# Graph layers on one core: ScalarE's share of the tile loads, and a fourth slot for them

## The reference

```python
# layer 0
u = par_u[0] * par_u[1] * (diag_u[:, None] * ego_u @ W_u) + ego_u   # nodes 0..2047
i = par_i[0] * par_i[1] * (diag_i[:, None] * ego_i @ W_i) + ego_i   # the other 3072
e = jnp.concatenate([u, i], axis=0)
h = adj @ (adj.T @ e)
out = (h - mu) * jax.lax.rsqrt(var + LN_EPS) * ln_gamma + ln_beta + res
x = _layernorm(x + out)
# layer 1 (K = 4)
Tx_prev1 = L_scaled @ x                 # L_scaled is adj
out = Tx_prev2 @ weight[0] + Tx_prev1 @ weight[1]
for k in range(2, K):
    Tx_curr = 2.0 * (L_scaled @ Tx_prev1) - Tx_prev2
    out = out + Tx_curr @ weight[k]
x = _layernorm(x + out + bias)
```

## Time and profile before

| | |
|---|---|
| median of 3 runs | 1394.04 us (1385.07 to 1394.7) |
| profiled execution | 1395.09 us, span 1393.3 us |
| TensorE busy | 1201.9 us (86%) |
| VectorE busy | 883.3 us (63%) |
| ScalarE busy | 181.7 us (13%) |
| moved by DMA | 371.78 MB, mean 267 GB/s |
| mean granted TensorE clock | 0.949 of full speed |

### The profile page before, as it was taken

One profiled execution on the slowest core, in us unless ns is written; L12 is line 12 of the kernel. 1 busy time (PEld: TensorE's weight loads), 2 busy tenths in 40 slices (PEclk: granted clock), 3 DMA queues, 4 the chain that ended last, 5 costly groups with the idle time before them and its releaser, 6 DMA issues.

```text
span 1393.3 us, 14444 instructions
## 1 busy us (share of the span) xinstructions
PE 1201.9 (86%) x5324; PEld 514.1 (37%) x5324; DVE 883.3 (63%) x940; ACT 181.7 (13%) x353; POOL 62.5 (4%) x98
## 2 busy tenths in 40 slices
PE   5789989979989889787497899999999999678785
PEld 4344444434444344333132333334434444122221
DVE  2467655765767667566366677666556666677783
ACT  1112212212212122130001001000010000010111
POOL 0820000000000000000000000000000000011111
PEclk9899999989999999998789999999999999989898
DMA  8999999999999999869799999999999999999992
GB/s 246 248 253 275 254 281 256 273 258 278 238 280 248 281 248 267 178 122 180 148 232 268 291 332 319 299 308 298 261 251 330 317 333 310 337 311 324 322 340 76
DMA packets 414968, 371.78 MB, mean 267 GB/s; under 512 B 12892, under 2 KB 413572, under 8 KB 414932
## 3 DMA queue, kind: packets, MB, share of 16 engines
q1 hardware_dynamic: 301332, 258.33, 70.7%
q10 hardware_dynamic: 110880, 110.11, 28.9%
q0 software_dynamic: 2720, 2.86, 1.0%
HBM read 369.94 MB, written 1.31 MB: 266 GB/s over the span
## 4 chain that ended last, share of the span: by engine, by line
PE 35%; SPq 34%; DMA 15%; DVE 9%; issue 4%; ACT 1%; ACTq 1%; POOL 0%; DVEq 0%
PE bank L1024 24%; SPq L312 21%; SPq L323 12%; DMA raw<-in_adj 8%; DMA shared<-in_adj 6%; DVE turned L452 5%; PE bank L1075 2%; PE bank L1037 2%; PE bank L1053 1%; DVE shared L452 1%; PE bank L884 1%; PE bank L1180 1%; PE bank L1087 1%; DVE stats L414 1%; ACTq L265 1%
## 5 line engine op out<-in xcount | busy, mean ns | idle before, releaser
L1024 PE MATMUL bank<-turned,terms 128*128 128x512 f32 x680 | 316.9, 619 | 44.6 <-DVE turned L452 44.0
L452 DVE STREAM_TRANSPOSE turned<-raw 128x2048 f32<-128x2048 f32 x93 | 213.2, 2301 | 130.0 <-DMA raw<-in_adj 76.4
L884 PE MATMUL bank<-shared 128*64 128x256 f32 x1600 | 224.3, 404 | 48.0 <-DMA shared<-in_adj 47.7
L472 DVE STREAM_TRANSPOSE shared<-shared 32x512 f32<-32x512 f32 x320 | 224.9, 703 | 25.0 <-ACT t_cols L692 20.6
L1024 PEld LDWEIGHTS bank<-turned,terms 128*128 128x128 f32 x680 | 131.5, 198 | 221.0 <-issue 189.5
L460 DVE STREAM_TRANSPOSE turned<-raw 128x2048 f32<-128x2048 f32 x40 | 92.4, 2311 | 164.8 <-PE bank L923 153.8
L923 PE MATMUL bank<-turned,t_quart 128*64 128x512 f32 x320 | 170.7, 620 | 14.7 <-DVE t_quart L482 14.7
L904 PE MATMUL bank<-scratch,t_cols 128*64 128x512 f32 x320 | 171.3, 618 | 0.4 <-ACT scratch L686 0.4
L884 PEld LDWEIGHTS bank<-shared 128*64 128x64 f32 x1600 | 103.9, 141 | 139.1 <-DMA shared<-in_adj 65.9
L452 DVE STREAM_TRANSPOSE turned<-shared 128x2048 f32<-128x2048 f32 x47 | 107.4, 2299 | 62.8 <-DMA shared<-in_adj 33.4
L686 ACT COPY scratch<-bank 128x512 f32<-128x512 f32 x160 | 93.8, 587 | 281.9 <-PE bank L896 281.9
(11 more groups left out here) (125 smaller groups left out, 639.5 us busy)
## 6 DMA issues: line engine op xcount, KB each, us to landing
shared<-in_adj SPq DMA_DIRECT2D x100, 1024.0 KB, 10.8
raw<-in_adj SPq DMA_DIRECT2D x140, 512.0 KB, 9.4
raw<-in_adj ACTq DMA_DIRECT2D x140, 512.0 KB, 11.1
raw<-in_adj SPq DMA_DIRECT2D x160, 256.0 KB, 7.7
shared<-in_adj SPq DMA_DIRECT2D x70, 512.0 KB, 9.7
shared<-in_adj ACTq DMA_DIRECT2D x70, 512.0 KB, 11.7
xq<-in_x POOLq DMA_DIRECT2D x40, 32.0 KB, 7.0
out<-scratch POOLq DMA_DIRECT2D x40, 32.0 KB, 5.1
```

The costliest lines, as they stand in the source:

```text
L452: nc.vector.transpose(turned[place].rearrange("p (c b i) -> p b c i", c=GB, i=Q32), part_of[:, all_tiles[n][1] % SPAN]).then_inc(tile_turn ...
L472: last = nc.vector.transpose(low_turned[Q32 * c:Q32 * (c + 1), :, :, Q32 * q:Q32 * (q + 1)], low[Q32 * q:Q32 * (q + 1), :, :, Q32 * c:Q32 ...
L884: last = nc.tensor.matmul(t_bank[H * odd:H * (odd + 1), 0:PW], e[:, s * SB + b, :], panels[slot][:, s * SB + b, :], start=(k == 0 and b < ...
L1024: last = nc.tensor.matmul(sum_bank[parity][:, :], terms[:, c * GB + i, columns], turned[place][:, i * BANK:(i + 1) * BANK], start=(first a ...
```

## The change

Three things. ScalarE issues its halves of units 1 and 2 right behind its last full copy for layer 0 (two calls of `load_next` in the loop), those of unit 3 behind root 3, and from root 4 on it calls `load_through`, which issues each unit whose slot is freed by a tile that VectorE turns ahead of that root's variance. There are four slots of 2 MB in place of three; unit u then waits for the last tile of unit u - 4. The fourth slot and unit 3 lie over layer 0's inputs and its last low block, so unit 3 waits until TensorE has read that block (`low_used`). To make room, the two further `turned` buffers move: one to another place in `shared`, one onto `xq`, which holds the residual input of the norms and is not read after the last of them.

```diff
-SLOTS = 3
+SLOTS = 4
...
-        pairs = [raw_base[:, 0:pair_size], raw_base[:, pair_size:2 * pair_size], shared[:, at:at + pair_size]]
-        turned += more[MORE_RAW:]
+        pairs = [raw_base[:, 0:pair_size], raw_base[:, pair_size:2 * pair_size], shared[:, at:at + pair_size],
+                 shared[:, at + pair_size + tile_size:at + 2 * pair_size + tile_size]]
+        turned += [shared[:, at + pair_size:at + pair_size + tile_size],
+                   xq.rearrange("p k f -> p (k f)")[:, 0:tile_size]]
...
-            return T1 + loads[u - SLOTS][2] if u >= SLOTS else (T1 - 3, T1 - 1, None)[u]
+            return T1 + loads[u - SLOTS][2] if u >= SLOTS else (T1 - 3, T1 - 1, None, None)[u]
...
-                if free_after(u) is None:
+                if u == 2:
                     sp.wait_ge(at_made, NJ * ITEMS)
+                elif u == 3:
+                    sp.wait_ge(low_used, NJ + 1)
...
-                if free_after(u) is None:
+                if u == 2:
                     act.wait_ge(at_made, NJ * ITEMS)
+                elif u == 3:
+                    act.wait_ge(low_used, NJ + 1)
...
+                    if (k, cc) == (TILED - 1, PB - 1):
+                        load_next()
+                        load_next()
                     if k >= 1:
                         (take_h, take_y)[cc](k - 1, SEGS[k - 1])
...
             load_next()
-            load_next()
             take_y(NS - 1, SEGS[-1])
             for n in range(4, 2 * NS):
-                while issued[0] <= load_of[max(0, n // 2 * 5 + n % 2 * 3 - 9)]:
-                    load_next()
+                load_through(n // 2 * 5 + n % 2 * 3 - 9)
                 root(n, 2 * GB)
```

More of the change, by code:

```diff
@@ L46 @@
 TURNED = 2
-MORE_RAW = 3
 MORE_TURNED = 2
@@ L106, in resnorm_chebyshev @@
         turned = [turned_base[:, k * tile_size:(k + 1) * tile_size] for k in range(TURNED)]
-        more = [shared[:, at + k * tile_size:at + (k + 1) * tile_size] for k in range(MORE_RAW + MORE_TURNED)]
         pair_size = SPAN * tile_size
-        pairs = [raw_base[:, 0:pair_size], raw_base[:, pair_size:2 * pair_size], shared[:, at:at + pair_size]]
-        turned += more[MORE_RAW:]
+        pairs = [raw_base[:, 0:pair_size], raw_base[:, pair_size:2 * pair_size], shared[:, at:at + pair_size],
+                 shared[:, at + pair_size + tile_size:at + 2 * pair_size + tile_size]]
+        turned += [shared[:, at + pair_size:at + pair_size + tile_size],
+                   xq.rearrange("p k f -> p (k f)")[:, 0:tile_size]]
         ident = sb("ident", [P, P])
```

## The result

The changed kernel takes 1311.4 us (median of 4, 1306.4 to 1329.4) beside 1389.6 for the kernel before in the same runs (median of 4, 1376.6 to 1394.7): a ratio of 0.944, interval 0.935 to 0.953. The forecast was 1337 with a range from 1322 to 1356. A second set gave 1322.1 against 1390.7, ratio 0.953 (0.943 to 0.963). A ratio leaves out executions over 1.5% above the fastest of their kernel; in one set (three to one, units 1 and 2 late, layer 0 on two queues, in the table further down) this leaves two of the seven of the kernel before, 1360.6 and 1374.1, and the three ratios come out 1.4 to 2 points above those of the medians.

A forecast was written before the change was run, and what follows sets the result against it. Late ScalarE load halves starve the first 20 tiles; loads bound the third sweep. 44 (first tiles) + 7 (first sweep) + 6 (third sweep) = 57 us off 1395.1 gives 1338, or 1337 as median; range 1322 to 1356.

The forecast's parts named there:

- The diagnosis: First 20 tiles: VectorE's transposes wait for ScalarE's load halves, issued late behind square roots; TensorE busy 68 of 104 us.
- Nothing is full there: First 20 tiles, 620 to 724 us: loads late although DMA engines have room, share 0.87 and 181 GB/s.
- First tiles, 44 us forecast: First 20 tiles: halves on time let tiles follow every 3.47 us, tile 19 at 679 instead of 723.93; 44 us less.
- The later start by up to 0.9 us: Before the first tiles: early issues of units 1 and 2 delay ScalarE's copies, root 1 and first norm up to 0.9 us.
- First sweep, 7 us: Rows after the first: fourth slot has units ready when row 2 begins, removing load waits; 7 us, between 4 and 9.
- Third sweep, 6 us: Load-bound third sweep: fourth slot gives only a lead fetched earlier, no faster loading by the unit; 6 us.
- one unit's lead: One more unit fetched ahead while TensorE bounds, paid out once when loads bind again; 6.0 us, 6.8 at 308 GB/s.
- Layer 0, 0 us: Layer 0, ahead of the sweeps' first tile: the sum had no term for it, 0 us.
- Only the halves on time count: Rival: later stages bound by bytes, so slots give nothing; 46 or 38 us off, 1348 to 1356; chance 0.17.
- More in flight lowers the rate: Rival: eight half units queued push the load rate down, 1407 us at 280 GB/s; chance 0.03 of over 1% slower.
- Roots held back: Rival: waits ahead of roots delay norm steps and tiles, first-tile gain shrinks to some 20 us; 1356 to 1375, chance 0.05.
- The rule of the Trainium skill: All issuers share 16 DMA engines, so moved issues save only issue time; result near 1390, no separate chance given.

The follow-up runs named there:

- three to one: Changed kernel, but SP issues three of the four DMAs of each unit and ScalarE one: 1578.0 us, ratio 1.155 to the kernel before.
- units 1 and 2 late: Changed kernel with ScalarE's halves of units 1 and 2 back behind root 3, the others on time: 1331.5 us, ratio 0.972.
- layer 0 on two queues: Changed kernel with layer 0's tile loads issued by ScalarE, so SP's queue carries only the panels there: 1275.7 us, ratio 0.934.
- on time alone: Kernel before with ScalarE's halves issued as soon as their slots are free, still three slots: 1347.5 us, ratio 0.973.
- depth 3 until then: Changed kernel, but units wait as with three slots up to the third sweep and with four in it: 1327.4 us, ratio 0.968.
- the four slots alone: Changed kernel with four slots, but ScalarE's halves in the old order around the roots: 1361.7 us, ratio 0.983.
- neighbours in one half: Changed kernel with SP issuing quarters 2 and 0, ScalarE 3 and 1, so both queues mostly write the same partition half: median 1532.0 us.

## Why the prediction was right in its sign and too small

- **The diagnosis held.** ScalarE's halves late behind the roots: on time alone takes the first stretch from 115.8 to 68.7 us. "Nothing is full there" was not so: one half of the partitions was served alone for 70% of the time, at 208 GB/s, near its limit, while the other stood.
- **First tiles, 44 us forecast:** 45.3 measured, by the forecast's own terms: 3.56 us a tile for 3.47 plus 1 in all. I had charged nothing for roots behind load issues; one stood 2.0 us, not for a slot but, as inferred above, for a full queue.
- **The later start by up to 0.9 us** did not show: tile 2 began right behind its norm step, at 596.95.
- **First sweep, 7 us:** 8.8, most of it in row 2, 36.2 to 29.8 us.
- **Third sweep, 6 us: the step of the mechanism that failed.** The sum took one unit's lead, and said "There a deeper queue makes nothing faster by the unit". The lead was there, 6 us by the runs and 1.2 units by the count. But at depth 3 the rate was not the engines' best: 327 GB/s at a share of 1.10, against 339 with four. That is the rest of the 13.3, some 7 to 8 us. The prediction's own rows had the gap: one unit every 6.04 us is 347 GB/s, while the stretch moved 319. I had read a share of 1.08 to 1.10 as full, and the room for the lead from the share too (1.09 against 1.12), which it does not measure. Time in which only one half of the partitions is served runs near 200 GB/s at a full share, and a fourth unit covers part of it: it is 7% of the third sweep with three slots, 4% in the changed kernel and 2% with depth 3 until then. By estimate the 5 points between first and last are half of the gain in rate (0.05 x 130 = 6.5 of 13 GB/s); why the rate with both halves served also rises, from 329 to 337, stays open.
- **Layer 0, 0 us: the term that put the result outside the range.** The sum left everything ahead of the first tile as it was, and the range held nothing for it. In the profiled pair it was 21.1 us, a difference between executions and not the change's. The profiled execution that the sum starts from, 1395.1, was at the slow end of the kernel's own 1376.6 to 1394.7 in that set. With the third sweep's 13 in place of 6 the forecast would have been 1330, still 19 above the result; by the stretches, 68 us off, it would have been 1327. The first set came out 78 us below before and the second 69, at 1322.1, just inside the range. That the first set's extra 10 us are layer 0's chance is argued: the later stretches repeat within 2 to 3 us, but not every execution has a trace.
- **Rivals.** "Only the halves on time count" is refuted by the four slots alone (0.983, and 8.7 and 14.6 us in the stretches that it left alone). "More in flight lowers the rate" is refuted: the rate rose. The low window of the earlier trace rows has another reason: only one half of the partitions was served in 60% of it, at 219 GB/s. "Roots held back" happened once, by 2.0 us. The rule of the Trainium skill, "DMA: Bandwidth & Descriptors", section "Issuing engines are not separate DMA queues", would have put the result near 1390, and it came out at 1311.

## What to carry to other kernels

Before trusting a DMA share near 1, divide bytes by time and ask which partitions are being written: with DMAs of 32 partitions give one queue the partitions 0 to 63 and the other 64 to 127, and let both always have work (338 GB/s against 217 to 224). In an in-order engine that also issues loads, put the issue where the slot becomes free, but small critical operations ahead of it: an issue with several DMAs outstanding took up to 4.45 us here, and moving the roots ahead gave 1.5 to 3. And before setting a range, compare the parts of the runs that the change does not touch: their spread belongs in it.

## What the hardware showed that I had not expected

- The rate at a DMA share of 1.10 to 1.13 was anywhere from 217 to 338 GB/s in stretches of 160 us and more, by the dealing of the same four DMAs alone: 217 (one queue), 220 (neighbours in one half), 224 (three to one), 338 in the third sweep with a half for each queue.
- An issue on ScalarE's queue took 4.45 us instead of 0.4 with the slot free and several DMAs outstanding. SP's, with all DMAs on it, took 19.3 us for 8, which is 217 GB/s, just as fast as they were carried out.
- Layer 0, on one queue with panels and tiles mixed, lasted until 587 to 611 us with the same code; with the tiles on the other queue, until 557 to 561. On the one queue its panels of 128 partitions moved at 348 GB/s and its tile loads of 32 partitions at 180 to 200.
